# A change in the order of the prologue and of the first tile: loads, checks of the operands, x2 transposes, sums, and the last two products

## The reference

```python
x = x + attn(layernorm(x))     # time mixing, k, v, r projections, a WKV scan over time, W_o
x = x + ffn(layernorm(x))

def ffn(x):
    h = silu(tlin(x, w1_w, w1_s)) * tlin(x, w2_w, w2_s)    # 256 -> 1024
    h = gelu(tlin(h, h1_w, h1_s))                          # 1024 -> 1024, exact gelu
    h = gelu(tlin(h, h2_w, h2_s))                          # 1024 -> 1024
    return tlin(h, w3_w, w3_s)                             # 1024 -> 256

def tlin(x, w, s):
    return einsum('bsi,oi->bso', x, w) * s                 # w holds -1, 0 and 1
```

## Time and profile before

| | |
|---|---|
| median of 3 runs | 1517.04 us (1515.98 to 1517.59) |
| the profiled execution | 1516.69 us, of which span 1515.0 us |
| TensorE busy | 1490.3 us, 98% of the span |
| VectorE busy | 1212.3 us, 80% |
| ACT busy | 1083.9 us, 72% |
| TensorE's mean granted clock | 0.995 of full speed |
| DMA moved | 290.52 MB, mean 192 GB/s |

### The profile page before, as it was taken

How to read it: one execution, slowest core, us unless ns; L and a number is a source line. 1 busy time by engine, 2 the same in 40 slices (tenths; PEclk the granted TensorE clock), 3 DMA queues, 4 the chain that set the end, 5 groups by cost and what they waited for, 6 DMA issues and landing times.

```text
span 1515.0 us, 28726 instructions
## 1 busy us (share of the span) xinstructions
PE 1490.3 (98%) x10292; PEld 1330.7 (88%) x10292; DVE 1212.3 (80%) x1594; ACT 1083.9 (72%) x1610; POOL 250.2 (17%) x512
## 2 busy tenths in 40 slices
PE   7899999999999999999999999999999999999998
PEld 5589889898998989989898998989899898998998
DVE  6777687887878798787888878789787878878664
ACT  5677586776877768686775877668686776868664
POOL 0301204021120311203021120301203031120300
PEclk9999999999999999999999999999999999999999
DMA  9897367474756737466574746737465573746653
GB/s 346 304 383 276 91 207 204 140 233 111 233 141 194 228 106 247 120 207 185 163 227 109 240 120 208 217 122 232 134 207 167 171 243 98 243 119 206 179 183 125
DMA packets 95758, 290.52 MB, mean 192 GB/s; under 512 B 9200, under 2 KB 33392, under 8 KB 93296
## 3 DMA queue, kind: packets, MB, share of 16 engines
q1 hardware_dynamic: 87568, 282.25, 57.2%
q0 software_dynamic: 8160, 7.87, 4.4%
HBM read 265.44 MB, written 36.18 MB: 199 GB/s over the span
## 4 chain that ended last, share of the span: by engine, by line
PE 92%; issue 2%; ACT 2%; POOL 0%; DVE 0%; POOLq 0%; ACTq 0%; DVEq 0%
PE acc L586 26%; PE acc L588 26%; PE att L516 10%; PE acc L560 7%; PE acc L561 7%; PE acc L614 4%; PE acc L616 4%; PE att L526 3%; PE att L495 2%; PE acc L661 1%; PE acc L663 1%; PE att L561 1%; PE att L560 1%; ACT early L1001 1%; ACT blocks L911 0%
## 5 line engine op out<-in xcount | busy, mean ns | idle before, releaser
L586 PE MATMUL acc<-op_hi,ring 128*128 128x256 f32 x3360 | 810.9, 286 | 1.4 <-DVE parts L1444 1.4
L588 PE MATMUL acc<-op_lo,ring 128*128 128x256 f32 x3360 | 788.9, 278 | 0.0
L586 PEld LDWEIGHTS acc<-op_hi,ring 128*128 128x128 f32 x3360 | 632.0, 188 | 19.8 <-issue 18.7
L588 PEld LDWEIGHTS acc<-op_lo,ring 128*128 128x128 f32 x3360 | 631.3, 188 | 11.1 <-issue 10.0
L1392 DVE TENSOR_TENSOR op_lo<-blocks,op_hi 128x1024 fp32r<-128x1024 f32 (+1 forms) x267 | 338.5, 1283 | 106.4 <-ACT op_hi L870 104.3
L870 ACT ACTIVATE op_hi<-blocks 128x1024 fp32r<-128x1024 f32 (+1 forms) x267 | 291.6, 1104 | 83.0 <-DVE blocks L1387 76.2
L560 PE MATMUL acc<-x_hi,w_rnd 128*128 128x512 f32 x448 | 178.6, 399 | 1.4 <-DVE blocks L1401 1.3
L1771 POOL TENSOR_TENSOR v_sb<-mix_v,v_sb 128x1024 f32<-128x1024 f32 (+1 forms) x17 | 39.1, 2299 | 852.5 <-DVE r_sb L1344 852.5
L561 PE MATMUL acc<-x_lo,w_rnd 128*128 128x512 f32 x448 | 177.2, 396 | 0.0
L911 ACT ACTIVATE blocks<-acc,vec 128x256 f32<-128x256 f32 x272 | 106.8, 478 | 75.0 <-PE acc L588 62.4
L911 ACT ACTIVATE blocks<-parts,vec 128x256 f32<-128x256 f32 x240 | 102.7, 499 | 57.5 <-DVE parts L1439 49.7
(11 more groups left out here) (143 smaller groups left out, 2128.2 us busy)
## 6 DMA issues: line engine op xcount, KB each, us to landing
ring<-scratch SPq DMA_DIRECT2D x436, 512.0 KB, 4.2
stage<-in_w_ffn SPq DMA_DIRECT2D x12, 1024.0 KB, 13.6
x_in<-in_x SPq DMA_DIRECT2D x32, 256.0 KB, 4.4
scratch<-in_w_ffn SPq DMA_DIRECT2D x8, 1024.0 KB, 15.7
scratch<-stage SPq DMA_DIRECT2D x8, 1024.0 KB, 7.0
out<-x_next SPq DMA_DIRECT2D x30, 256.0 KB, 5.0
out<-mix_v POOLq DMA_DIRECT2D x30, 256.0 KB, 4.4
w_plain<-in_w_ffn SPq DMA_DIRECT2D x3, 1024.0 KB, 19.9
```

Of the source, the lines that this page charges most:

```text
L586: pe.matmul(out, act(w), act(op_hi[:, k, c, :]), start=(begins and c == 0 and m % 2 == 0), stop=False, skip_group_check=True)
L588: mm = pe.matmul(out, act(w), act(op_lo[:, k, c, :]), start=False, stop=(c == QC - 1), skip_group_check=True)
```

## The change

Seven things are done to the order, and none to what is computed.

1. SP: `wm` is issued right behind the vectors, then the four blocks of h1, W1 and W2 to `w_plain`, then s3, which gets a semaphore of its own (`ld_s3`), waited for by VectorE only behind the first flag.
2. SP: W1 and W2 are loaded into `w_rnd` as soon as both are in `w_plain`; W3 goes to `w_plain` behind them, and into `w_rnd` only after the h2 blocks are copied to scratch.
3. ACT: the checks of the prologue stand in another order, and W3's check moves from the prologue into the first tile and from the first flag to the flag of the sums. 10 pieces make the first flag, 9 the second.
4. TensorE: the transposes of `FIRST[0]`'s x2 stand ahead of the two warm products behind the flag's matmul.
5. VectorE: `block_sum(0, 0)` moves from the begin of the first tile to behind `lo23(0, 1)`.
6. First tile: `plain(1,2)` and `plain(1,3)` take s=1 first, then s=0; the gelu of the output (1,1,1) waits for a semaphore set by `plain(1,3)` s=1 (`pe_c22`); `ln2(WHOLE, 1)` stands ahead of `gelu_plain(1,1,0)`.
7. TensorE: `last(0, ...)` is moved behind the branch on the flag of the sums, as it reads W3.

```diff
-        RAW_CHECKS, SUM_CHECKS = 3 + 2 * 4, 2 * 4
+        RAW_CHECKS, SUM_CHECKS = 2 + 2 * 4, 1 + 2 * 4
...
             sp.dma_start(vec[:], vectors).then_inc(ld_const, 16)
-            load_area(A21_)
             sp.dma_start(wm[:], w_mix).then_inc(ld_const, 16)
-            load_area(A22_)
-            sp.dma_start(s3_row[:], s3.broadcast_to([P, D])).then_inc(ld_const, 16)
-            load_area(A11_)
-            load_area(A12_)
+            for k in range(4):
+                load_area(k)
             for n, a in enumerate((0, W12)):
                 sp.dma_start(w_plain[n], w_ffn[:, a:a + W12]).then_inc(st_w, 16)
+            sp.dma_start(s3_row[:], s3.broadcast_to([P, D])).then_inc(ld_s3, 16)
             for k in range(4):
                 sp.dma_start(STAGED[k], raw_block(1, k)).then_inc(ld_raw2, 16)
-            sp.dma_start(w_plain[2], w_ffn[:, 2 * W12 + 2 * HH:]).then_inc(st_w, 16)
-            sp.wait_ge(st_w, 16 * 3)
-            for n, a in enumerate((W1_AT, W2_AT, W3_AT)):
+            sp.wait_ge(st_w, 16 * 2)
+            for n, a in enumerate((W1_AT, W2_AT)):
                 sp.dma_start(w_raw[:, a:a + W12], w_plain[n]).then_inc(ld_w, 16)
+            sp.dma_start(w_plain[2], w_ffn[:, 2 * W12 + 2 * HH:]).then_inc(st_w3, 16)
...
                 to_scratch(1, step, raw_block(1, k), st_blocks[1])
+            sp.wait_ge(st_w3, 16)
+            sp.dma_start(w_raw[:, W3_AT:W3_AT + W3], w_plain[2]).then_inc(ld_w3, 16)
             keep_x1(0)
...
-                            if s == 1:
+                            if s == seqs[-1]:
                                 pe_half.add(mm)
+                        if l == 1 and block == 3 and s == 1:
+                            mm.then_inc(pe_c22, 1)
...
                     plain(1, 1)
-                    plain(1, 2)
+                    plain(1, 2, (1, 0))
                     project_out(WHOLE, 1)
...
-                    plain(1, 3)
-                    pe.wait_ge(flag_max, 2)
-                    last(0, lambda: transpose_x2(WHOLE, 1), True)
-                    pe.sem_inc(pe_half.sem, HALF_STEPS - PLAIN_STEPS)
+                    plain(1, 3, (1, 0))
...
+                last(0, lambda: transpose_x2(WHOLE, 1), True)
+                pe.sem_inc(pe_half.sem, HALF_STEPS - PLAIN_STEPS)
...
-            pe.wait_ge(ld_const, 16 * 3)
+            pe.wait_ge(ld_const, 16 * 2)
...
-            keep_warm(WARM[5], w_k)
-            for n, s in enumerate(FIRST):
-                transpose_x2(s, 0)
+            transpose_x2(FIRST[0], 0)
+            keep_warm(WARM[5], w_k, BANK[6])
+            transpose_x2(FIRST[1], 0)
...
-                act.wait_ge(pe_half.sem, pe_half.at(0, 8 * l + 4 * row + 4))
+                if (l, row, s) == (1, 1, 1):
+                    act.wait_ge(pe_c22, 1)
+                else:
+                    act.wait_ge(pe_half.sem, pe_half.at(0, 8 * l + 4 * row + 4))
...
             check_raw(0, A21_)
+            check_raw(0, A22_)
             for n, s in enumerate(FIRST):
                 copy_kvr(s, 0, range(DC))
-            check_raw(0, A22_)
+            check_raw(0, A11_)
...
-            check_raw(0, A11_)
+            check_raw(0, A12_)
...
-            check_raw(0, A12_)
-            for k in range(3):
-                check_raw(1, k)
+            check_weight(W1_AT)
+            check_weight(W2_AT)
+            check_raw(1, 0)
             copy_x1(FIRST[0], 0)
+            check_raw(1, 1)
+            check_raw(1, 2)
+            copy_x1(FIRST[1], 0)
             check_raw(1, 3)
-            check_weight(W1_AT)
-            copy_x1(FIRST[1], 0)
-            check_weight(W2_AT)
             ln2(FIRST[0], 0)
-            check_weight(W3_AT)
             ln2(FIRST[1], 0)
...
                 hi_plain(0, 1, 1)
+                check_weight(W3_AT)
                 copy_kvr(WHOLE, 1, [5])
...
                 hi_plain(1, 1, 1)
+                ln2(WHOLE, 1)
                 gelu_plain(1, 1, 0)
                 hi_plain(1, 1, 0)
-                ln2(WHOLE, 1)
...
             def first_tile():
-                block_sum(0, 0)
                 dve.wait_ge(ld_x.sem, ld_x.at(1))
...
                 lo23(0, 1)
+                block_sum(0, 0)
                 block_sum(0, 1)
```

More of the change, by code:

```diff
@@ L277, in build @@
         ld_first = [ctx.enter_context(nc.semaphore(f"ld_first{n}")) for n in range(n_seq)]
-        ld_w = ctx.enter_context(nc.semaphore("ld_w"))
+        ld_w, ld_w3, st_w3 = (ctx.enter_context(nc.semaphore(n)) for n in ("ld_w", "ld_w3", "st_w3"))
+        pe_c22 = ctx.enter_context(nc.semaphore("pe_c22"))
         ld_raw1 = [ctx.enter_context(nc.semaphore(f"ld_raw1_{k}")) for k in range(4)]
@@ L282, in build @@
         sums = [ctx.enter_context(nc.semaphore(f"sums{l + 1}")) for l in range(2)]
+        ld_s3 = ctx.enter_context(nc.semaphore("ld_s3"))
         st_blocks = [ctx.enter_context(nc.semaphore(f"st_blocks{l + 1}")) for l in range(2)]
@@ L988, in hi_plain @@
                 act.wait_ge(ready.sem, ready.at(0, (l + 1) * QC))
-                act.wait_ge(pe_half.sem, pe_half.at(0, 8 * l + (6, 8)[row]))
+                if (l, row, s) != (1, 1, 1):
+                    act.wait_ge(pe_half.sem, pe_half.at(0, 8 * l + (6, 8)[row]))
                 hi(PLAIN_OPERANDS[row][s], ALL, done)
@@ L1007, in check_weight @@
             def check_weight(a):
-                check_piece(w_raw[:, a:a + W12], (ld_w, 16 * 3))
+                check_piece(w_raw[:, a:a + W12], (ld_w3, 16) if a == W3_AT else (ld_w, 16 * 2))
             def check_sum(l, k):
@@ L1546, in _ @@
             reciprocal_deviation(s, 0, range(NB))
-            dve.wait_ge(ld_const, 16 * 3)
+            dve.wait_ge(ld_const, 16 * 2)
             dve.wait_ge(setup_pool, 2)
@@ L1573, in _ @@
             set_flag(0, BANK[0], RAW_CHECKS)
+            dve.wait_ge(ld_s3, 16)
             for n, s in first_parts:
```

## The result

The changed kernel takes 1521.02 us (median of 13 runs, 1519.85 to 1522.64) against 1516.73 us for the kernel before (13 runs, 1515.9 to 1517.89): ratio 1.0028, 95% interval 1.002 to 1.0037. The profiled execution took 1521.89 us, with a span of 1520.2 us. In it TensorE is busy 1491.7 us, 1.4 us more than before (a matmul at half clock counts as busy for longer); the rest of the 5.2 us by which the span grew is idle time, and the question is where it lies.

What follows compares the result with a forecast made beforehand. TensorE, busy 98%, was taken to bound the kernel; -0.8+0+2.1+3.74-1.7+0+2.4, rounded to +5.8, on the profiled 1516.69 gave 1522.5, and 0.35 for the median made 1522.8 us. Range 1519.2 to 1525.3.

Steps and rivals of the forecast that it cites:

- Prologue -0.8: Ahead of the loop: ACT's checks end earlier, so the first tile's gate starts at 63.9, 0.8 us earlier.
- W2 at 43.0: Prologue loads: W1 and W2 queue behind the staged blocks, so W2 lands at 43.0, against 50.4 for all three before.
- six checks and two copies: ACT in the prologue: its work from W2's landing at 43.0 takes 13.1 us, done at 56.1.
- Sums 0: VectorE, first tile: the x load's landing covers the removed sum, and the later sums cost 0; without cover up to 4.7 us.
- W3's check +2.1: First tile: one more piece in ACT's gapless run moves the gelu's release from 141.81 to 143.91, +2.1 us.
- Swap +3.74: `plain(1,2)`: s=1 first waits for `act_g12`'s gelu without s=0 as cover, +3.74 us.
- Waits in `last` -1.7: First tile's end: C22 finished earlier and `ln2` ahead of the last gelu remove waits of 0.24 and 1.11 us, -1.7.
- Clock +2.4: Behind the wait of 6.65 us in `plain(1,2)`, TensorE runs at half rate for 4.6 to 5.3 us, +2.4.
- Rival 1: `plain(1,2)`: the stall comes but the clock holds, 1520.4 us; chance 0.11.
- Rivals 2 and 3: Prologue: W shares engines with staged blocks, W2 by 40.2, 1518.9, chance 0.10; or W comes later, 1525.3, chance 0.10.
- Rivals 4 and 5: First tile: swap not felt, `act_g12` set before 137.3, 1516.6, chance 0.04; or that with early W, 1512.7, chance 0.03.

Runs made afterwards that it cites:

- the experiment: Changed kernel with W3's check moved into the stretch before the first gelus, where ACT waits for TensorE: 1518.97 us, against 1521.35 for the changed kernel timed again.
- the pair with and without warm products: Changed kernel with seven warm products, which nobody reads, put in the wait ahead of `plain(1,2)`: 1519.24 us; the changed kernel timed again without them: 1521.35 us.
- the repeat: The changed kernel as it is, timed again beside three variants of it on one chip: 1521.35 us, against 1516.51 for the kernel before.
- the best version: Changed kernel, `plain(1,2)` s=0 first, W3's check in ACT's gap, ACT's staged checks first, six more warm products before the flag's matmul, none between transposes: 1507.35 us.
- first tile of 100.67 us: Changed kernel with `plain(1,2)` back to s=0 first and W3's check in ACT's gap: 1513.57 us, against 1515.90 for the kernel before.
- the last but one kernel of the table: Changed kernel, `plain(1,2)` s=0 first, W3's check in ACT's gap, ACT's staged checks first, no warm products between transposes, none added before the flag's matmul: 1510.39 us.

## Why the prediction held

The forecast was 1522.8 us, slower, by a stall of `plain(1,2)` with a slow clock behind it. It came out slower, 1521.02, within the range. By its terms:

- **Prologue -0.8.** 0.0 in the trace after, a mean of -0.7 over the seven kernels with this prologue and ACT's order unchanged (gate 0 from 63.40 to 64.77) against the mean of the three with the old one (63.66 to 65.81), and -0.6 in the medians. None of these is told from nothing, so this gain is neither shown nor refuted. W2 at 43.0: seen at 42.56 to 43.71 over the seven, and at 43.56 in the trace after, where it put the flag's matmul at 56.74 instead of 56.2. The step that was off is the chain behind the flag: the transposes were taken at 0.75 us each group, a mix of clocks, and ran at 1.1 at half clock. (The six checks and two copies sum to 13.4 us by the prediction's own terms, not 13.1; they took 13.0.)
- **Sums 0.** Held: VectorE waited for x all the same, and no wait of TensorE came of it.
- **W3's check +2.1.** 1.87 us of wait (the 1.88 us by which ACT's gelus moved, 1.86 less in the experiment), and taking it out brings 0.9 us of clock with it.
- **Swap +3.74.** 3.73 us of wait (6.25 - 2.52), 3.71 in the kernel before alone.
- **Waits in `last` -1.7.** -1.9 and -1.7 in two pairs of traces that differ by the swap of `plain(1,3)` and the place of `ln2`, the two causes that the prediction named. My later idea that a delay would cover them fell.
- **Clock +2.4.** 2.1 by the pair with and without warm products. After the wait of 6.25 us the clock was back 5.1 us behind the restart, and 4.7 in the repeat, both in the range used.

The terms as measured give -0.7 + 1.9 + 3.7 - 1.9 + 2.1 = 5.1 us; the medians say 4.3 (13 runs) and 4.8 (8 runs), and the intervals of the ratios reach from 3.0 to 5.6 and from 2.7 to 5.9 us, so the rest isn't told from nothing. Of the 1.8 us by which the forecast was too high, 0.3 us is the median of before, 1517.04 in three runs and 1516.73 in thirteen, 0.7 us the terms, and 0.8 us lies between the terms and the medians.

Rival 1 (the clock holds) would have given 1520.4, which the medians alone couldn't have ruled out; the trace and the warm products do. Rivals 2 and 3 needed W2 before 40.2 or 2.45 us later than 43.0: it came 0.6 us later in the trace after, and from 0.4 earlier to 0.7 later over the seven. Rivals 4 and 5 needed a gelu 6.6 us earlier; it wasn't.

## What to carry to other kernels

Before products are reordered, ask what the other order's first operand waits for and what the old order did meanwhile: here one swap cost 3.7 us and its neighbour brought 1.9, in one edit that measured as one number. A wait on the engine that bounds the kernel is to be priced with the slow clock behind it, and where it can't be removed, work that nobody reads can buy that part back. An engine that checks or converts incoming data should take it in the order in which it lands: of the 8.4 us by which the best version beats the kernel before, 2.8 came with that order and 3.3 with warm products at the right place.

## What the runs showed of the hardware

The half clock's price doesn't grow evenly with the wait. Taking the first tile of 100.67 us with a wait of 0.6 as the base and the longer wait off, it is 2.3 and 2.1 us behind 6.25 us, 1.2 behind 4.38 and 1.4 behind 2.52 (whose first tile holds 0.3 us of another wait, taken off too). Each is one trace, and the two with 6.25 us differ by 0.2, so 1.2 and 1.4 aren't told apart. What I had not known is that a part was due behind 2.5 us of idle time already, since the trace of before had no wait between 1.7 and 4.20 us. In that one trace the clock fell 2.4 us into the wait; in the others it fell later, 3.3 us into the prologue's wait of the kernel before and 4.6 us into the wait of 6.25 us. Whether it falls behind 2.5 us in every execution isn't shown. In the prologue the clock stayed at half for up to 7.3 us behind the restart (53.8 to 61.1 in the last but one kernel of the table), in the first tile for 5.1, with gaps in the one and a full TensorE in the other.
